# Nearest-neighbour attention on one Trainium2 core: both heads transposed in one run, scores in two banks, distances two steps sooner

## The reference

```python
x2 = sum(x * x, -1)
d2 = x2[:, :, None] + x2[:, None, :] - 2 * einsum('bnc,bmc->bnm', x, x)
d2 = d2 + big * eye(N)
_, idx = top_k(-d2, 32)                 # each row's 32 nearest rows
q, k, v = split(x @ Wqkv, 3)            # 8 heads of 64 channels
dots = einsum('bhnd,bhmd->bhnm', q, k) * SCALE
attn = softmax(where(adj, dots, -inf))
out = h + einsum('bhnm,bhmd->bhnd', attn, v) @ Wout + bout    # x is the layer-normed h
```

## Time and profile before

| | |
|---|---|
| time, median of 3 runs | 4313.74 us (4312.88 to 4317.17) |
| profiled execution, its own time | 4316.81 us |
| its span | 4315.0 us |
| PE / DVE / ACT / POOL busy, whole program | 88% / 66% / 54% / 46% |
| first scores of this stage | 2556 us from the span's start |
| last start of its scores' reading by DVE | 3678 us |

### The profile page before, as it was taken

One profiled execution on the slowest core, in us unless ns is written; L12 is line 12 of the kernel. 1 busy time (PEld: TensorE's weight loads), 2 busy tenths in 40 slices (PEclk: granted clock), 3 DMA queues, 4 the chain that ended last, 5 costly groups with the idle time before them and its releaser, 6 DMA issues.

```text
span 4315.0 us, 110651 instructions
## 1 busy us (share of the span) xinstructions
PE 3815.2 (88%) x31697; PEld 2606.8 (60%) x31697; DVE 2862.9 (66%) x9352; ACT 2339.5 (54%) x5933; POOL 1974.2 (46%) x2276
## 2 busy tenths in 40 slices
PE   7488857697999799999897869999999999899999
PEld 7355533485666566666685546666666666555555
DVE  2577738785888644444465878888888887455554
ACT  5455525322444344444343548888888888455555
POOL 0143428674656412222474645555555555344333
PEclk9999967797999899999655879999999999999999
DMA  2111124331111323333112310000000001233332
GB/s 54 36 31 30 30 31 113 90 83 39 38 36 38 72 67 81 81 80 80 29 38 46 71 37 12 11 11 11 11 11 11 11 11 27 64 74 75 78 76 57
DMA packets 465512, 203.02 MB, mean 47 GB/s; under 512 B 435090, under 2 KB 455566, under 8 KB 465170
## 3 DMA queue, kind: packets, MB, share of 16 engines
q1 hardware_dynamic: 465298, 200.65, 20.5%
HBM read 154.67 MB, written 45.91 MB: 46 GB/s over the span
## 4 chain that ended last, share of the span: by engine, by line
PE 54%; issue 17%; POOL 14%; DVE 9%; SPq 2%; ACT 2%; DMA 2%; POOLq 0%; DVEq 0%; ACTq 0%
POOL att_P L3576 8%; PE sw_pH L4180 5%; PE moe_pH L2726 5%; PE sw_pY L4167 5%; PE moe_pY L2749 4%; DVE att_M L1177 3%; PE att_pS L982 3%; PE moe_pH L2730 3%; PE moe_pH L2736 2%; POOL att_norm_rstd L673 1%; PE att_pS L2219 1%; PE att_pO L1044 1%; PE ret_pR L1836 1%; PE att_pO L3039 1%; PE att_pP L3685 1%
## 5 line engine op out<-in xcount | busy, mean ns | idle before, releaser
L3576 POOL TENSOR_TENSOR att_P<-att_P,att_rden 125x498 f32<-125x498 f32 x512 | 520.3, 1016 | 514.6 <-DVE att_rden L3871 514.1
L3764 ACT ACTIVATE att_P<-att_Z,att_nb 125x249 f32<-125x249 f32 x1024 | 501.5, 494 | 22.4 <-DVE att_nb L3883 20.7
L2791 DVE TENSOR_TENSOR moe_hT<-moe_silu,moe_pH 128x498 f32<-128x498 f32 x384 | 258.8, 674 | 312.8 <-ACT moe_silu L2775 312.8
L4228 ACT ACTIVATE sw_hT<-sw_pH,sw_b 128x498 f32<-128x498 f32 x512 | 317.8, 672 | 220.9 <-PE sw_pH L4180 220.9
L3685 PEld LDWEIGHTS att_pP<-att_ident,att_P 124*125 124x125 f32 (+1 forms) x2048 | 262.6, 187 | 233.8 <-issue 233.8
L3685 PE MATMUL att_pP<-att_ident,att_P 124*125 124x124 f32 (+1 forms) x2048 | 349.8, 293 | 49.7 <-issue 28.9
L3883 DVE CUSTOM_DVE_ANT_0 att_Z<-att_pS,att_mask 125x249 f32<-125x249 f32 x1024 | 366.0, 413 | 29.9 <-PE att_pS L3673 27.9
L2775 ACT ACTIVATE moe_silu<-moe_pH 128x498 f32<-128x498 f32 x384 | 225.1, 586 | 263.0 <-PE moe_pH L2730 177.1
L3771 ACT ACTIVATE att_PTr<-att_pP 125x498 f32<-125x498 f32 x512 | 296.6, 579 | 102.2 <-PE att_pP L3685 94.7
L2702 POOL TENSOR_TENSOR moe_xe<-moe_share,moe_x 128x1992 f32<-128x1992 f32 x32 | 130.0, 4064 | 430.8 <-DMA moe_share<-mixing 380.5
L4087 POOL TENSOR_TENSOR sw_acc<-sw_acc,sw_Z 128x249 f32<-128x249 f32 x224 | 154.1, 688 | 365.2 <-DVE sw_Z L4307 364.4
(11 more groups left out here) (463 smaller groups left out, 9697.2 us busy)
## 6 DMA issues: line engine op xcount, KB each, us to landing
moe_share<-mixing SPq DMA_DIRECT2D x64, 498.0 KB
sw_share<-mixing SPq DMA_DIRECT2D x64, 498.0 KB, 5.5
ffn_W<-in_ffn_pairs SPq DMA_DIRECT2D x64, 192.0 KB, 2.4
att_F<-h_stream SPq DMA_DIRECT2D x192, 62.5 KB
att_X<-h_stream SPq DMA_DIRECT2D x192, 62.5 KB
h_stream<-att_H SPq DMA_DIRECT2D x64, 62.5 KB
ffn_F<-h_stream SPq DMA_DIRECT2D x64, 62.5 KB
ret_F<-h_stream SPq DMA_DIRECT2D x64, 62.5 KB
```

Source lines behind the costliest of these rows:

```text
L3576: g.tensor_tensor(own, own, bc(rden[:, j % 2, c, :], T), ALU.mult).then_inc(*scaled.one())
L3764: ins = a.activation(P[:, r, c, t, :], Z[:, r, c, t, :], ACT.Exp, scale=-1.0, bias=nb[:, r, c, t:t + 1], accum_out=den[:, r, c, t:t + 1])
L4228: a.activation(hT[:, k % 4, :, :], pH[:, place, :, 0:T], ACT.Relu, bias=b1[:, k:k + 1]).then_inc(*hid_ready.one())
```

## The change

Transposes: both heads are transposed in one run of eight at place 3 into two banks of `pP`, and ACT evicts both banks with one instruction of 996 columns at place 4. Their waits are halved in number: a run waits for the scale of head 1 and for the eviction of the step before. `pS` shrinks to two banks, so the scores of a step wait for DVE's reading of the step just before. DVE's reciprocal of head 0 moves from place 0 to place 2, behind the first reading of scores.

V moves on TensorE from place 5 of steps 2 and 3 to place 2 of steps 5 and 7, the distances from place 5 of step 7 to place 2 of step 6, the transposes of `xn` from place 5 of step 6 to place 3 of step 4. The turned output goes to place 3 of step 5. It and the transposes of `xn` get a bank of their own, `pX`. `near` gets two buffers and is written in step 6. POOL's small operations for the next rows move from place 5 of steps 1, 2, 4, 5 and place 1 of step 7 to place 5 of step 0 and place 1 of steps 1, 2, 3 and 5. DVE's spread moves from step 3 to step 1. ACT evicts the output at place 2 of steps 3 and 7.

```diff
-        near = st.sb("near", [PT, 2, 2, T])
+        near = st.sb("near", [PT, 2, 2, 2, T])
@@
-        pS = st.psum("pS", [PT, 4, 512])
-        pP = st.psum("pP", [128, 512])
+        pS = st.psum("pS", [PT, 2, 512])
+        pP = st.psum("pP", [PT, 2, 512])
         pO = st.psum("pO", [128, 512])
+        pX = st.psum("pX", [128, 512])
@@ gpsimd, pre
-                if place == 5:
-                    if s == 1:
-                        g.wait_ge(*xn_ready.before(n))
-                        norm.center(g, n, g4(F[:, u, :, :, :]))
-                    if s == 2:
-                        norm.square(g, n)
-                    if s == 4:
-                        norm.power(g, n)
-                    if s == 5:
-                        g.wait_ge(*xT_done.before(n))
-                        norm.scale(g, n, g4(xn[:, :, :, :])).then_inc(*xn_ready.one())
-                if s == 7 and place == 1:
+                if s == 0 and place == 5:
+                    g.wait_ge(*xn_ready.before(n))
+                    norm.center(g, n, g4(F[:, u, :, :, :]))
+                if s == 1 and place == 1:
+                    norm.square(g, n)
+                if s == 2 and place == 1:
+                    norm.power(g, n)
+                if s == 3 and place == 1:
+                    g.wait_ge(*xT_done.before(n))
+                    norm.scale(g, n, g4(xn[:, :, :, :])).then_inc(*xn_ready.one())
+                if s == 5 and place == 1:
                     g.wait_ge(*xT_ready.after(n))
@@ tensor
-                if s == 6:
+                if place == 3 and s == 4:
                     pe.wait_ge(*xn_ready.after(n))
-                if s == 7:
+                if place == 2 and s == 6:
                     pe.wait_ge(*sq_ready.after(n))
-                    if since(n, 3):
-                        pe.wait_ge(*h_ready.after(n - 3))
+                    pe.wait_ge(*v0_ready.after(n - 1, 0))
+                    pe.wait_ge(*v1_ready.after(n - 1, 0))
-                if place == 5 and s in (2, 3):
-                    t = s - 2
-                    pe.wait_ge(*qk_ready.after(n, s))
+                if place == 2 and s in (5, 7):
+                    t = (s - 5) // 2
+                    if t == 0:
+                        pe.wait_ge(*qk_ready.after(n))
+                    else:
+                        pe.wait_ge(*v0_ready.after(n, 0))
+                        pe.wait_ge(*v1_ready.after(n, 0))
+                        pe.wait_ge(*latest(near_ready, n + 1))
@@
-                pe.wait_ge(*max_ready.after(n, 2 * (s - 2) + 1))
+                pe.wait_ge(*max_ready.after(n, 2 * (s - 1) + 1))
-            def turn(n, j, c):
-                pe.wait_ge(*scaled.after(n, 2 * j + c))
-                pe.wait_ge(*pt_ready.after(n, 2 * j + c - 1))
+            def turn(n, j):
+                pe.wait_ge(*scaled.after(n, 2 * j + 1))
+                pe.wait_ge(*pt_ready.after(n, j - 1))
                 st.held(pe)
-                for t in range(2):
-                    for kt in range(2):
-                        ins = pe.transpose(pP[0:PT, kt * T + t * OFF:kt * T + t * OFF + ROWS[t]],
+                for c in range(2):
+                    for t in range(2):
+                        for kt in range(2):
+                            ins = pe.transpose(pP[:, c, kt * T + t * OFF:kt * T + t * OFF + ROWS[t]],
@@
-                if place in (0, 3) and s >= 2:
-                    turn(n, s - 2, place // 3)
+                if place == 3 and s >= 2:
+                    turn(n, s - 2)
@@ scalar
-            def evict(n, j, c):
-                a.wait_ge(*pt_done.after(n, 2 * j + c))
+            def evict(n, j):
+                a.wait_ge(*pt_done.after(n, j))
                 a.wait_ge(*o_done.after(n, j - 2))
-                a.activation(PTr[:, j % 2, c, :], pP[0:PT, 0:2 * T], ACT.Copy).then_inc(*pt_ready.one())
+                a.activation(PTr[:, j % 2, :, :], pP[:, :, 0:2 * T], ACT.Copy).then_inc(*pt_ready.one())
@@ vector
-                if s == 3:
+                if s == 1:
                     norm.spread(v, n, 1e-5)
-                if s == 7:
+                if s == 6:
                     v.wait_ge(*d_done.after(n))
-                    v.wait_ge(*mask_ready.before(n))
+                    if since(n, 2):
+                        v.wait_ge(*mask_ready.after(n - 2))
-                if place in (0, 3) and s >= 1:
-                    invert(n, s - 1, place // 3)
+                if place in (2, 3) and s >= 1:
+                    invert(n, s - 1, place - 2)
```

More of the change, by code:

```diff
@@ L3601, in _ @@
                         pe.matmul(pQ[o, c, at], wT[r, 0, hp, :], wT[r, 1, hp, :], start=True, stop=True)
-                    for c, bank in ((0, pP), (1, pO)):
+                    for c, bank in ((0, pX), (1, pO)):
                         r = slice(c * D, (c + 1) * D)
@@ L3610, in pre @@
                 s, place = divmod(x, PLACES)
-                if place != 5:
-                    return
-                if s == 6:
+                if place == 3 and s == 4:
                     pe.wait_ge(*xn_ready.after(n))
-                    pe.wait_ge(*qk_ready.after(n - 1))
+                    if since(n, 4):
+                        pe.wait_ge(*h_ready.after(n - 4))
+                    pe.wait_ge(*xT_ready.before(n))
                     st.held(pe)
                     for t in range(2):
-                        ins = pe.transpose(pQ[:, 0, t * OFF:t * OFF + ROWS[t]],
+                        ins = pe.transpose(pX[:, 256 + t * OFF:256 + t * OFF + ROWS[t]],
                                            xn[0:ROWS[t], t, :, :].rearrange("p b c -> p (b c)"),
@@ L3642, in proj @@
                         pe.wait_ge(*near_ready.after(n))
[L3643 to L3646, removed]
+                        pe.wait_ge(*v0_ready.before(n))
+                        pe.wait_ge(*v1_ready.before(n))
+                    else:
                         pe.wait_ge(*qk_ready.after(n, s - 1))
@@ L3742, in pre @@
                 s, place = divmod(x, PLACES)
-                if place == 5 and s == 6:
+                if place == 5 and s == 4:
                     a.wait_ge(*xT_done.after(n))
-                    a.activation(xT[:, u, :], pQ[:, 0, 0:T], ACT.Copy).then_inc(*xT_ready.one())
+                    a.activation(xT[:, u, :], pX[:, 256:256 + T], ACT.Copy).then_inc(*xT_ready.one())
             def proj(n, u, x):
@@ L3752, in proj @@
                                  ACT.Copy).then_inc(*qk_ready.one())
-                if place == 5 and s in (2, 3):
+                if place == 3 and s in (5, 7):
+                    t = (s - 5) // 2
                     if since(n, 2):
                         a.wait_ge(*o_done.after(n - 2))
-                    a.wait_ge(*v_done.after(n, s - 2))
-                    a.activation(V[:, u, s - 2, 0, :], pQ[0:PT, 0, :], ACT.Copy).then_inc(*v0_ready.one())
+                    a.wait_ge(*v_done.after(n, t))
+                    a.activation(V[:, u, t, 0, :], pQ[0:PT, 0, :], ACT.Copy).then_inc(*v0_ready.one())
             def exps(n, j, c):
@@ L3782, in main @@
                     exps(n, s - 1, place // 2)
-                if place in (1, 4) and s >= 2:
-                    evict(n, s - 2, place // 4)
-                if place == 5 and s == 6:
+                if place == 4 and s >= 2:
+                    evict(n, s - 2)
+                if place == 2 and s == 7:
                     outputs(n, 0)
@@ L3791, in post @@
                     exps(n, STEPS - 1, place // 2)
-                if place in (1, 4) and s < 2:
-                    evict(n, s + STEPS - 2, place // 4)
-                if place == 5 and s == 2:
+                if place == 4 and s < 2:
+                    evict(n, s + STEPS - 2)
+                if place == 2 and s == 3:
                     outputs(n, 1)
@@ L3853, in proj @@
                 if place in (1, 4):
-                    select(n, s, place // 4)
-                if place == 5 and s in (2, 3):
+                    select(n, u, s, place // 4)
+                if place == 5 and s in (5, 7):
+                    t = (s - 5) // 2
                     if since(n, 2):
                         v.wait_ge(*o_done.after(n - 2))
-                    v.wait_ge(*v_done.after(n, s - 2))
-                    v.tensor_copy(V[:, u, s - 2, 1, :], pQ[0:PT, 1, :]).then_inc(*v1_ready.one())
+                    v.wait_ge(*v_done.after(n, t))
+                    v.tensor_copy(V[:, u, t, 1, :], pQ[0:PT, 1, :]).then_inc(*v1_ready.one())
                 if place == 5 and s == 7:
@@ L3863, in proj @@
                     v.wait_ge(*rounds.after(n))
-                    v.tensor_scalar(mask[:, u, :, :, :], near[:, :, :, :], TAKEN, NEG, ALU.not_equal,
+                    v.tensor_scalar(mask[:, u, :, :, :], near[:, u, :, :, :], TAKEN, NEG, ALU.not_equal,
                                     ALU.mult).then_inc(*mask_ready.one())
```

48 lines of the change are left out of this document (26 added, 22 removed).

## The result

The changed kernel takes 4251.67 us, median of 4 runs (4246.73 to 4252.6), beside 4315.3 for the kernel before in the same rounds. The ratio is 0.9851, 95% interval 0.9833 to 0.9868: faster by 1.5%. The forecast was 4254, in a range of 4232 to 4300.

The account below looks back on a forecast made before the run. TensorE, busy 95%, was taken as the bound, with waits on other engines. A pass falling from 35.49 to 33.61 saves 48.9 over 26, other passes 11.5: 4316.81 - 60 - 3.07 = 4254 us, range 4232 to 4300.

Parts of the forecast that it names:

- A change of kind costs 0.20 us: TensorE loses 0.20 us whenever it switches between full-array, row-half and column-half tiles.
- One change fewer a step, 1.60 a pass; V and distances, 0.60: TensorE: merged transposes save 8 x 0.20 us a pass; V and distances behind scores save three more changes.
- Idle marks as the sign of a change: TensorE's weight loads: idle marks of 0.32 or 0.37 us precede another tile kind; 24 a pass expected, not 35.
- The single bank's waits go: Head 1's transposes no longer wait for head 0's eviction, removing most of the 2.05 us of waiting a pass.
- ACT's eviction: 995 ns, nothing on the end: One ACT eviction of 996 columns takes 995 ns; saves at most 1.3 us of ACT a pass, none of the end.
- Scores in two banks: 1.33 to the read, 1.62 back: DVE first reads 1.33 us after scores start; the next scores may start 1.62 us after that read.
- the slower rival: Two-bank hand-off decides every step: 39.7 us a pass, +135 us, 4449; chance 0.09.
- the 0.12 for which I had it hold step 2: DVE's hand-off of score banks was to delay step 2's scores on TensorE by 0.12 us.
- POOL holds steps 2 and 3 by 0.52 and 0.83: POOL's small work between the heads' scales delays TensorE's transposes by 0.52 us in step 2, 0.83 in step 3.
- After the branch 1.8 us, all of it on TensorE: DVE idles about 1.8 us at step 0 after each loop branch; all reaches TensorE, so every second pass is 34.51.
- hid most of that: In the kernel before, four score banks hid most of DVE's 2.8 us pause after the loop's branch.
- The sum: 26 middle passes save 48.9 us, five other passes 11.5, the last nothing; 60 in all, giving 4254.

Follow-up runs that it names:

- experiments 1 and 2: Changed kernel with an always satisfied wait between the two heads' transposes: 4254.81 us; with a tiny row-half matmul there and no wait: 4329.88 us.
- experiment 10: Changed kernel with the heads' transposes and evictions in two runs again, each head with its own bank: 4258.9 us.
- experiment 3: Changed kernel with POOL's square, power and scale of the next rows moved to place 5 of steps 0, 1 and 2: 4212.71 us.
- Experiment 8: Changed kernel with V made behind the values again, at place 5 of steps 5 and 7, instead of behind the scores: 4308.7 us.
- experiment 9: Kernel before the change with 28 passes in the loop's body, so no branch is taken in the stage: 4300.31 us, ratio 0.995.
- q3_two_runs: The kernel of experiment 10: changed kernel with the transposes in two runs again, each head with its own bank: 4258.9 us.
- experiment 7: Changed kernel with ACT's eviction of 996 columns split into two of 498, signalled together at the end: 4249.2 us.
- p1_pool: The kernel of experiment 3: changed kernel with POOL's small work moved out from between the two heads' scales: 4212.71 us.

## Why the prediction was right, point by point

- *A change of kind costs 0.20 us.* Shown (experiments 1 and 2).
- *One change fewer a step, 1.60 a pass; V and distances, 0.60.* Both are shown by lengths. The merging: 3.71 a step with two runs (experiment 10) and 3.52 with one (3009.23 to 3012.75 in experiment 3). V: scores with V behind them take 1.90 to the transposes and scores alone 1.04, so V costs 0.86 where it cost 1.06; the distances, 2.72 to the transposes in step 6, cost 1.68 where they cost 1.88 (scores at 3045.98, transposes at 3048.70). Experiment 8 doesn't test this, as V keeps its neighbours' kind there.
- *Idle marks as the sign of a change.* This reading was wrong, though nothing in the sum hangs on it. I wrote that a mark stands before each load that follows another kind, and expected 24 a pass instead of 35. Values follow transposes, another kind, without a mark, in the earlier trace rows already; the loads stand idle only 0.12 us there (2986.42 to 2986.54), too little for the view to mark. It marks some 17 a pass now and 20 before. The price of a change is read from start to start.
- *The single bank's waits go.* The kernel before waits 34.78 - 33.44 = 1.34 us a pass apart from its branch (experiment 9), and in q3_two_runs, where each head has its bank, passes without a branch have none: 32.91 against 32.84 of work. Of the 1.34, 1.22 was the bank and 0.08 the distances (experiment 9). The distances moved from step 7 to step 6, one step and not two as the title has it; x's transposes moved two.
- *ACT's eviction: 995 ns, nothing on the end.* 1001 ns, and at most 0.09 us a pass on the end (experiment 7).
- *Scores in two banks: 1.33 to the read, 1.62 back.* 1.33 and 1.60. The hand-off decides after the branch only, so the slower rival had no ground; the 0.12 for which I had it hold step 2 is not there (steps 0 and 1 last 3.52 where no branch is near).
- *POOL holds steps 2 and 3 by 0.52 and 0.83.* 0.33 and 0.94, and both vanish when its work is moved. The sum, 1.27 for 1.35, was right; DVE came some 0.3 sooner than I had it, in part because the mask takes 0.67 in its new place, not 0.83. Why it is shorter there is not known.
- *After the branch 1.8 us, all of it on TensorE.* 1.9 to 2.1 in most passes, 2.0 on average; in the one shown 1.64 in step 0 and 0.23 more in step 2's transposes. Right in size. Beside it I wrote that four banks "hid most of that", of DVE's 2.8, before. The kernel before hid half of it, 1.4, and the changed one hides 0.8 (experiment 9); whether the banks or something else makes the difference was not tested. This did not enter the sum, which compares measured passes before with worked-out ones after.
- *The sum.* 47.7 for 48.9 in the middle, 13.1 for 11.5 at the ends, 60.8 for 60.4. Some of this closeness is luck: passes without a branch are 32.64 where I had 32.71, the branch costs 2.0 where I had 1.8, and the two errors partly cancel, as do those of the middle and the ends. That 4254 met 4251.67 to 2.3 us is luck too, as the executions of the changed kernel alone span 5.9 us.

In one thing the working misleads: it lists 1.60 as a gain of the merging and 1.35 as a cost of POOL's places, and I read them, until experiment 10, as separate. They are one trade. What paid in the changed kernel as it stands was the rest: a bank for each head (1.22 of waiting) and V and distances beside the scores (0.60), together the 1.8 us by which a pass is shorter, with one run or with two. The merging pays where POOL's work is out of its way.

## What to carry to other kernels

When two waits are merged into one, the work behind both waits for the later; put nothing between the producers of the two, and look for it on the slowest of them. Price a pass by going once round the ring with each engine's own order, since busy shares (95, 83 and 81% here) can't tell a 1.6 us gain from one that is given back. Undo the part that looks most valuable on its own before believing its share.

## What the runs showed that was not expected

A taken branch costs by the length of the loop's body, engine by engine: 0.2 us for TensorE and ACT and 2.8 for DVE with two passes in the body, 3.2 to 3.8 for TensorE and ACT and 3.1 for DVE with four, where the whole ring loses 7.4 us a branch on average. Unrolling by two made the kernel 17 us slower, unrolling altogether made p1_pool 22 us faster. A neighbouring pass is a poor measure of a branch: in the kernel before, the pass after that also carried part of it.
